# Transformer block on one core: set-up rebuilt, prepared layouts from the host, inverse roots moved to GpSimd

## The reference, cut to what matters

```python
x = x + layernorm(attn(layernorm(x)))          # no scale, no shift, eps 1e-5
x = x + layernorm(moe(layernorm(x)))

# attn
q, k, v = x @ Wq, x @ Wk, x @ Wv               # (2, 16 heads, 1024, 64)
logits = q @ k.T + causal + pos_bias           # pos_bias[h, i, j] = rel[h, clip(127 - (i - j), 0, 127)] for j <= i
out = softmax(logits / 64) @ v
return concat_heads(out) @ Wo + bo

# moe
shared = gelu(x @ Wfc_s + bfc_s) @ Wproj_s + bproj_s
routed = sum over e of (gelu(x @ Wfc[e] + bfc[e]) @ Wproj[e] + bproj[e]) * gate[:, e]
```

## Time and profile before

| what | value |
|---|---|
| time, median of 3 runs | 875.44 us (874.59 to 875.71) |
| span of the profiled execution | 874.6 us |
| time of the profiled execution itself | 874.59 us, the lowest of the three |
| busy: PE, PEld | 775.7 us (89%), 661.3 us (76%) |
| busy: DVE, ACT, POOL | 716.2 us (82%), 624.6 us (71%), 265.7 us (30%) |
| chain that ended last | PE 70%, DVE 12%, ACT 6%, issue 5%, DMA 4% |
| DMA | 71.74 MB, mean 82 GB/s |

### The profile page before, as it was taken

One profiled execution on the slowest core, in us unless ns is written; L12 is line 12 of the kernel. 1 busy time (PEld: TensorE's weight loads), 2 busy tenths in 40 slices (PEclk: granted clock), 3 DMA queues, 4 the chain that ended last, 5 costly groups with the idle time before them and its releaser, 6 DMA issues.

```text
span 874.6 us, 17078 instructions
## 1 busy us (share of the span) xinstructions
PE 775.7 (89%) x4453; PEld 661.3 (76%) x4453; DVE 716.2 (82%) x1610; ACT 624.6 (71%) x1366; POOL 265.7 (30%) x285
## 2 busy tenths in 40 slices
PE   2988299999999999999999999998379999999993
PEld 2667288888888888888888888887367877777772
DVE  6648088888888888888888888888869899999886
ACT  2557177877887787787778778778386776667764
POOL 2220223323332332332332233222401344444421
PEclk9999699999999999999999999999779999999997
DMA  8769534324423423432442342341001221122101
GB/s 218 261 227 111 76 72 93 78 60 89 91 60 84 95 61 69 93 78 60 88 92 60 84 95 61 69 92 50 31 1 48 76 73 72 72 72 72 49 1 48
DMA packets 61993, 71.74 MB, mean 82 GB/s; under 512 B 40020, under 2 KB 50960, under 8 KB 58896
## 3 DMA queue, kind: packets, MB, share of 16 engines
q1 hardware_dynamic: 56944, 67.73, 30.9%
q0 software_dynamic: 720, 2.12, 2.9%
q10 hardware_dynamic: 4304, 1.58, 0.8%
HBM read 28.35 MB, written 9.53 MB: 43 GB/s over the span
## 4 chain that ended last, share of the span: by engine, by line
PE 70%; DVE 12%; ACT 6%; issue 5%; DMA 4%; ACTq 1%; DVEq 0%; POOL 0%; SPq 0%; POOLq 0%
PE out_ps L1214 16%; PE trans_ps L1196 15%; PE score_ps L1181 12%; PE shared_ps L1226 6%; DMA q_hl<-k_hl 3%; DVE pT_lo L973 3%; PE score_ps L1086 3%; PE score_ps L1088 3%; PE score_ps L1087 3%; DVE pT_lo L873 3%; ACT pT_hi L670 2%; PE trans_ps L1086 2%; PE trans_ps L1088 2%; PE trans_ps L1087 2%; PE shared_ps L1086 2%
## 5 line engine op out<-in xcount | busy, mean ns | idle before, releaser
L670 ACT ACTIVATE pT_hi<-trans_ps 128x512 fp32r<-128x512 f32 (+3 forms) x384 | 185.8, 493 | 77.8 <-PE trans_ps L1196 38.0
L655 ACT ACTIVATE probs<-score_ps,row_min 128x128 f32<-128x128 f32 (+7 forms) x256 | 190.4, 744 | 53.1 <-DVE row_min L860 52.8
L873 DVE TENSOR_TENSOR pT_lo<-trans_ps,pT_hi 128x512 fp32r<-128x512 f32 (+3 forms) x384 | 202.0, 554 | 31.1 <-ACT pT_hi L670 29.6
L860 DVE CUSTOM_DVE_ANT_0 score_ps<-score_ps,bias 128x128 f32<-128x128 f32 (+7 forms) x256 | 194.4, 759 | 39.3 <-PE score_ps L1181 36.6
L1196 PE MATMUL trans_ps<-ident,probs 128*128 128x128 f32 x1152 | 191.1, 275 | 20.1 <-DVE pT_lo L873 19.8
L1181 PE MATMUL score_ps<-k_hl,q_hl 128*128 128x512 f32 (+2 forms) x768 | 183.6, 353 | 19.7 <-DMA k_hl<-k_hl 19.1
L467 POOL TENSOR_TENSOR acc<-acc,head_out 128x512 f32<-128x512 f32 x64 | 82.4, 1288 | 316.8 <-DVE head_out L891 288.3
L1196 PEld LDWEIGHTS trans_ps<-ident,probs 128*128 128x128 f32 x1152 | 138.0, 141 | 44.4 <-DVE pT_lo L873 28.0
L1181 PEld LDWEIGHTS score_ps<-k_hl,q_hl 128*128 128x128 f32 x768 | 135.1, 189 | 40.8 <-issue 19.5
L1214 PE MATMUL out_ps<-pT_hi,v_hl 128*128 128x512 f32 (+2 forms) x384 | 156.8, 409 | 1.1 <-DVE pT_lo L873 1.1
L973 DVE TENSOR_TENSOR pT_lo<-probs,pT_hi 128x512 fp32r<-128x512 f32 x144 | 133.1, 953 | 23.8 <-ACT pT_hi L732 15.6
(11 more groups left out here) (135 smaller groups left out, 1156.2 us busy)
## 6 DMA issues: line engine op xcount, KB each, us to landing
q_hl<-k_hl SPq DMA_DIRECT2D x64, 256.0 KB, 3.6
k_hl<-k_hl SPq DMA_DIRECT2D x32, 512.0 KB, 4.2
v_scratch<-probs SPq DMA_DIRECT2D x16, 512.0 KB, 3.1
v_raw<-v_scratch SPq DMA_DIRECT2D x32, 256.0 KB, 4.5
bias_all<-gate_scratch SPq DMA_DIRECT2D x8, 1024.0 KB, 4.9
bias_all<-bias_scratch SPq DMA_DIRECT2D x1, 2048.0 KB, 9.1
v_raw<-in_L_ffn_Wfc SPq DMA_DIRECT2D x8, 256.0 KB, 4.8
bias<-in_L_ffn_Wproj SPq DMA_DIRECT2D x8, 256.0 KB, 5.1
```

The costliest lines, as they stand in the source:

```text
L655: act.activation(probs[s % 4][:, 0:n], scores_of(s % QB)[:, 0:n], ACT.Exp, bias=row_min[:, s:s + 1], scale=-1.0, accum_out=row_sum[:, s:s ...
L670: act.activation(pT_hi[c][:, CH * g:CH * g + m, q * P:(q + 1) * P], trans_ps[k % 2][:, 0:m * P].rearrange("p (m q) -> p m q", q=P), ACT.Co ...
L860: dve.tensor_tensor_reduce(out=ps, in0=ps, in1=bias_b[b][:, T - n:T], scale=1.0, scalar=3e38, op0=ALU.add, op1=ALU.min, accum_out=row_min[ ...
L873: dve.tensor_tensor(pT_lo[c][dst], trans_ps[k % 2][:, 0:m * P].rearrange("p (m q) -> p m q", q=P), pT_hi[c][dst], ALU.subtract).then_inc(p ...
```

## The change

The host now hands over arrays in the layout in which they are used: `Wqk` (per head q beside k), `Wo2` (Wo by head, repeated for both halves of the partitions), `rel_steps` (the relative bias already spread over 128 x 256 positions per head, in the right order), and `layer_bias` (expert biases, transposed). On the chip:

- SP loads x, `Wqk`, `rel_steps` (head 0, then the others), `Wo2`, `Wr` and `layer_bias` before the first store. The DRAM round trip of the bias, POOL's DMAs, the exchange matrix with its eight matmuls and ACT copies, and PE's transpose of the expert biases are gone.
- POOL shapes the bias of each head (`shape_bias`): it subtracts the first column, scales, and masks. Head 0's is done in set-up, head s's in slot s of head 0.
- The output bias is loaded once for each partition (64 KB) and POOL spreads it over `acc` in two copies, in slots 2 and 7 of head 0.
- The inverse root is one POOL instruction, variance to the power -0.5; the DVE reciprocal is gone, the Newton step stays. ACT no longer uses its square root.
- The low part of Wv is made by DVE behind the first normalised piece, no longer by POOL.

```diff
+            def root(n, lo, hi):
+                pool.wait_ge(var_ready, norms_to(n, lo))
+                pool.tensor_tensor(rstd[:, lo:hi], var_eps[:, lo:hi], minus_half[:, lo:hi], ALU.pow).then_inc(root_ready, 1)
...
+            def shape_bias(h):
+                then_wait(pool.tensor_scalar(bias_all[:, h, :], bias_all[:, h, :], far[:, h:h + 1], SCALE,
+                                             ALU.subtract, ALU.mult))
+                near = bias_all[:, h, P:2 * P]
+                then_wait(pool.affine_select(out=near, in_=near, compare_op=ALU.is_ge, fill=MASKED, base=0,
+                                             pattern=[[-1, P]], channel_multiplier=1))
...
@@ pool, slot @@
-                if s == QB - 2 and not carried:
-                    for r in range(2):
-                        pool.dma_start(wo[r * DH:(r + 1) * DH, :, :],
-                                       Wo.rearrange("(h d) n -> d h n", h=H)).then_inc(wo_loaded, 16)
-                    pool.dma_start(acc[:], bass.AP(bo.tensor, 0, [[0, P], [0, NB], [1, D]])).then_inc(acc_started, 16)
+                if s == 0 and not carried:
+                    pool.wait_ge(bias_loaded[1], 16)
+                    then_wait(pool.tensor_copy(far[:, 1:H], bias_all[:, 1:H, 0]))
+                elif not carried:
+                    shape_bias(s)
+                if s in (2, QB - 1) and not carried:
+                    b = s // (QB - 1)
+                    pool.wait_ge(bo_loaded, 16)
+                    pool.tensor_copy(acc[:, QB * b:QB * (b + 1), :],
+                                     bo_all[:].unsqueeze(1).broadcast_to([P, QB, D])).then_inc(acc_started, 1)
@@ sync @@
+            load_x(0)
+            load_x(1)
+            sp.dma_start(wqk[:], Wqk).then_inc(wqk_loaded, 16)
+            load_x(2)
+            load_x(3)
+            sp.dma_start(bias_all[:, 0:1, :], rel_steps[:, 0:1, :]).then_inc(bias_loaded[0], 16)
+            sp.dma_start(bias_all[:, 1:H, :], rel_steps[:, 1:H, :]).then_inc(bias_loaded[1], 16)
+            sp.dma_start(wo[:], Wo2).then_inc(wo_loaded, 16)
...
@@ scalar @@
-            act.dma_start(rel[:], rel_pos_bias).then_inc(rel_loaded, 16)
             act.dma_start(wv[:], Wv).then_inc(wv_loaded, 16)
-            act.dma_start(wqk[:, :, 0:DH], Wq.rearrange("p (h d) -> p h d", h=H)).then_inc(wqk_loaded, 16)
-            act.dma_start(wqk[:, :, DH:2 * DH], Wk.rearrange("p (h d) -> p h d", h=H)).then_inc(wqk_loaded, 16)
+            act.dma_start(bo_all[:], bass.AP(bo.tensor, 0, [[0, P], [1, D]])).then_inc(bo_loaded, 16)
...
-            root(0, 0, CH)
+            act.wait_ge(ident_ready, 1)
+            act.activation(warm[:], ident[:, 0:1], ACT.Exp)
@@ vector, inverse_std @@
-                dve.wait_ge(std_ready, norms_to(n, lo))
-                then_wait(dve.reciprocal(r, std[:, lo:hi]))
+                dve.wait_ge(root_ready, norms_to(n, lo))
@@ vector, set-up, piece 0 @@
+                if c == 0:
+                    dve.wait_ge(wv_hi_done, 1)
+                    dve.tensor_tensor(wv_lo, wv[:], wv_hi, ALU.subtract).then_inc(wv_split, 1)
@@ tensor, set-up @@
-                    pe.matmul(trans_ps[n % 2][:], exchange[:], bias_flat[:, n * W:(n + 1) * W],
-                              start=True, stop=True).then_inc(bias_turn_psum, 1)
```

More of the change, by code:

```diff
@@ L57, in transformer_block @@
     SCALE = -1.0 / DH
-    assert (P, D, R, DH, B, NC) == (128, 128, 128, 64, 2, 2)
+    NORMS = ([(0, CH * c) for c in range(NCH)] + [(n, QB * b) for b in range(B) for n in (1, 2)]
+             + [(3, CH * c) for c in range(NCH)])
+    norms_to = lambda n, lo: NORMS.index((n, lo)) + 1
+    assert (P, D, DH, B, NC) == (128, 128, 64, 2, 2)
     LAG_PE = 2
@@ L143, in transformer_block @@
         ident = sb("ident", [P, P])
-        exchange = sb("exchange", [P, P])
+        bo_all = sb("bo_all", [P, D])
         stats = sb("stats", [P, NB, 6])
@@ L219, in transformer_block @@
         wo_loaded = sem("wo_loaded")
-        rel_loaded = sem("rel_loaded")
+        bo_loaded = sem("bo_loaded")
+        acc_started = sem("acc_started")
         small_loaded = sem("small_loaded")
[L222 to L225, removed]
+        bias_loaded = [sem(f"bias_loaded{i}") for i in range(2)]
+        var_ready = sem("var_ready")
+        root_ready = sem("root_ready")
         ident_ready = sem("ident_ready")
@@ L572, in _ @@
                         split_wfc(0, 0)
+                        root(2, 0, QB)
                     add_head(H - 1, *WO_SLOT[s])
+            root(1, QB, NB)
             split_wproj(0, 0)
+            root(2, QB, NB)
             split_wfc(1, 1)
@@ L626, in _ @@
             copy_v(1)
-            root(0, 3 * CH, 4 * CH)
             nT_evac(0, 2)
@@ L721, in _ @@
                 nT_evac(1, c)
-            root(1, QB, NB)
             def hidden_units(e, c):
@@ L742, in hidden_units @@
                         high(k - 1)
[L744 to L746 removed]
+            act.wait_ge(small_loaded, 16 * 2)
             hidden_units(0, 0)
[L748 removed]
             normalise_moe_in(1)
@@ L1393 @@
     nc = _bacc.Bacc("TRN2", target_bir_lowering=False, num_devices=1)
+    g = {k.replace("L0_attn_", "").replace("L0_ffn_", ""): _np.asarray(v)
+         for k, v in inputs.items()}
+    heads, head = g["rel_pos_bias"].shape[0], g["Wq"].shape[1] // g["rel_pos_bias"].shape[0]
+    width = g["Wq"].shape[0]
+    g["Wqk"] = _np.concatenate([g[n].reshape(width, heads, head) for n in ("Wq", "Wk")], axis=2)
+    by_head = g["Wo"].reshape(heads, head, width).transpose(1, 0, 2)
+    g["Wo2"] = _np.concatenate([by_head, by_head], axis=0)
+    span = g["rel_pos_bias"].shape[1]
+    steps = _np.clip(_np.arange(2 * span)[None, :] - _np.arange(span)[:, None] - 1, 0, span - 1)
+    g["rel_steps"] = g["rel_pos_bias"][:, steps].transpose(1, 0, 2)
+    g["layer_bias"] = _np.concatenate([g["bfc_s"].reshape(-1, width), g["bfc"].reshape(-1, width),
+                                       g["bproj_s"].reshape(1, width), g["bproj"]], axis=0).T
     arrays, args = {}, []
     for name in _INS:
-        a = _np.ascontiguousarray(inputs[name])
+        a = _np.ascontiguousarray(g[name])
         arrays[f"in_{name}"] = a
         args.append(nc.dram_tensor(f"in_{name}", a.shape, _mybir.dt.from_np(a.dtype), kind="ExternalInput").ap())
-    shape = inputs["L0_attn_x"].shape
+    shape = g["x"].shape
     args.append(nc.dram_tensor("out_0", shape, _mybir.dt.float32, kind="ExternalOutput").ap())
```

129 lines of the change are left out of this document (37 added, 92 removed).

## The result

The changed kernel takes 861.17 us (median of 4 runs, 859.92 to 862.50) where the kernel before takes 875.58 (median of 4): ratio 0.984, 95% interval 0.983 to 0.985, a gain of 14.4 us. The forecast was 844.4, a gain of 31, and its range began at 837 and ended at 858. The direction was right and the gain is clear of noise; its size was forecast twice too large.

The account below looks back on a forecast made before the run. PE bounds the heads, but stands before head 1 while the 1 MB output-bias broadcast holds the q and k copies. Terms -20.2 - 4.8 - 4.5 - 0.5 + 1.8 - 2.8 = -31.0 from 874.6 give 843.6, median 844.4; range 837 to 858.

Parts of the forecast that it names:

- Output bias: Before head 1: without the 1 MB broadcast, PE's 18.5 us idle time and a half clock of 1.7 go; 20.2 gained.
- Front of set-up: Normalising x's first pieces: no wait for ACT's root, no reciprocal, POOL's Wv split moved to DVE; 4.8 us gained.
- I take 0.35 plus 0.1: In set-up: a POOL power priced at 0.35 us plus 0.1 to be noticed, near a small two-input instruction's 0.20.
- The rival that set-up gives nothing: 5.5 MB ahead of SP's first store arrive late, so gains of 4.8 and 4.5 go: 853.7 us, chance 0.11.
- The exchange: End of the V stage: eight matmuls of 0.86 us go, but stores set the pace; 4.5 us gained, not 6.9.
- POOL in head 0: Bias steps of 1.6 us delay head 1's weights, so PE stands in slot 8; 1.8 us lost.
- The rival with 2.5 us for a step: Head 0: slower bias steps make POOL the bound, weights of heads 1 and 2 late: 855.5 us, chance 0.15.
- The middle: Between attention and experts: offset 1.3 earlier, root's table load -1.5, POOL's splits cost 1.3, reload -1.3; 2.8 us gained.
- The end: After the last products: replacing root and reciprocal by a power changes nothing, 0 us.
- a power about as much: At the kernel's end: root and reciprocal cost 0.27 + 0.18 us, and a power was taken to cost about that.
- The rival of the slow power: About nine exposed roots: at 3.8 us a power uses up the 31.0 gain, at 6 us 895; chance 0.04.
- signs of being wrong: Whole kernel: a power over 1 us, head 0 longer than 35 us, or stores holding PE until 48.

Follow-up runs that it names:

- the clean run: The kernel before with only the output bias changed, its 64 KB loaded on SP's queue behind the load of `bias_all`: 855.55 us, ratio 0.978.
- the subtraction run: The changed kernel with a subtraction in place of the power in all twelve roots, giving other numbers: 851.16 us, ratio 0.971.
- tested alone: The changed kernel with eight float32 128x512 matmuls put back into PE's V stage, on other data: 862.94 us, ratio 0.984, slot 0 3.2 later.

## Why the forecast was wrong, step by step

- **Output bias: right.** Forecast 20.2; the clean run shows 21.0 at the attention statistics and 19.2 by the medians. The k copy at head 1 was in time, as worked out.
- **Front of set-up: mis-sized, by the power and by a load.** Forecast 4.8, first V matmul 2.2 earlier (15.98 for 18.16). The step "I take 0.35 plus 0.1" took the power as nearest to a small two-input form; it was 1.02, with DVE idle 1.1 to 1.2 for it. Two pieces make 1.6 us, as the subtraction run shows (second piece normalised at 12.41 instead of 14.05). The other part was not in the sum: x's first piece is 1.6 later because Wv is issued beside it. The rival that set-up gives nothing blamed the wrong loads, those behind x.
- **The exchange: mechanism right, the size a little off.** Forecast 4.5 with ends 2 and 6.9, and 3.0 when tested alone. At slot 0 the changed kernel shows only 2.4 for front and exchange together; with the roots back on ACT it is 53.15 - 46.10 = 7.1 of the 9.3, so the power and the clock took 4.7 there. That a longer idle time ahead of the last piece could bring the lower clock was missing in the forecast.
- **POOL in head 0: right.** Step forecast 1.6, measured 1.70 (60.81 to 62.51); PE's wait forecast 1.8, measured 2.4. The rival with 2.5 us for a step falls. The Trainium skill's rule for one-input work (GPSIMD Engine Reference, 4.1 Engine selection: roughly line rate) does not hold for this form: 1.15 us for 128x256 where a copy of that shape takes 0.40. Not forecast were the k copy's wait of 1.6 and that the idle time in head 0 can bring a half clock of 1.7 us.
- **The middle: the sign was wrong.** Forecast 2.8 gained, 1.5 of it up to the second normalising, and 1.8 lost there. The forecast's own gains were real: with the subtraction the middle takes 27.5, that is 2.0 less than before. Up to the first normalising it is 15.29 before and 13.64 then, 1.65 less where the forecast had 1.3 for the first offset; from there to the second 14.17 and 13.84, 0.3 less where it had 1.5 for the table load less 1.3 for POOL's splits. Those splits do lie on the Newton steps (1.11 and 0.52 where 0.17 is their own); with the roots back on ACT they don't, which pays there for the load that came back. The failed step is again the power, here 1.64 us on eight columns and four times: 2.1 us up to the first normalising (15.70) and 1.7 from there to the second (15.56). The Trainium skill (ScalarE: Activation LUTs, What ACT_TABLE_LOAD costs) adds 1.38 us of drain to each switch. The trace does not show it: with the roots on ACT an activation ends at 618.26, the load runs from 618.28 to 619.56, and the root starts at 619.57.
- **The end: "a power about as much" failed.** From the last gated product but one 15.8 us instead of 14.3; 13.5 with the subtraction. Between middle and end another 0.8 went, and the reload's 1.3 with it. From the second normalising to the last gated product but one it is 212.2 to 212.6 us in the kernel before and the two runs with the output bias alone, and 213.0 to 214.5 in those of the changed kernel and its versions; in the first profile the reload's gain was there for a while: the first gated product behind the second normalising comes 38.1 us after it, and 39.0 before the change; by the fifth it is 62.8 against 62.4. PE is busy at full clock in between. No run was made for the cause, and it stays open.
- **The rival of the slow power** had the right mechanism with the wrong price: it asked for 3.8 us before all gain was gone. With the measured 1.02 to 1.64 the same count of nine exposed ones takes 9 x (1.02 - 0.35) = 6 to 9 x (1.64 - 0.35) = 11.6 us; taking it away gave 7.1 and 10.0. Of the forecast's own signs of being wrong two came, a power over 1 us and a V stage that ends behind 48 (slot 0 at 50.78). Head 0 stayed under 35 in the first of the changed kernel's two profiles, at 34.45, and not in the second.

The missing 14.5 us by place: 6.9 up to slot 0, 0.7 from there to the attention statistics, 3.3 in the middle, 2.1 from there to the last gated product but one (open), 1.5 at the end. By cause the shares overlap, and the first is by the medians: some 7 to 10 the power with the clock that follows it, 1.5 to 2 Wv beside x, 1.5 the smaller gain of the exchange.

## What to carry to other kernels

A price that no row bounds from above is not taken at its nearest cheap row when it stands nine times on the path; price it by the count at which it would use up the gain, and ask for a run of it first. An operation that is moved between engines for a cause seen in one place (a table load) should be moved in that place only: here the loads it saved cost less than its ten exposed executions. When two executions of one kernel differ by a fall of the clock, compare landmarks between traces that both have it or both lack it. And when one edit removes a stall of 20 us, measure that edit alone, or the losses of the others hide under it.

## What the runs showed of the hardware

- A power on POOL: 1.02 us for 128x4, 1.64 for 128x8, against 0.2 for a sum or product of that size. Two operations with a value per partition on 128x256: 1.15 us, where a copy of that shape takes 0.40.
- A fall of PE's clock to 1.2 GHz cost 1.5 us in the V stage and 1.7 in head 0, in some executions of one kernel and not in others. Of two executions with the same front, one had it after 2.75 us of idle time and the other not after 2.95.
- x's first piece (256 KB) landed at 3.8 with a load of 4 KB issued beside it on the other queue, at 5.4 to 5.8 with 512 KB in large rows, and at 7.8 with 64 KB that repeat one row of 512 B for 128 partitions: the small broadcast delayed it most.
